# A graph network on one core: a GpSimd share of the one-hot rows, loads ahead of stores, and quarters of sums ahead of one-hot products

## The chip, the cores and the metric

The kernel runs on one core of a Trainium2 chip. The metric is the device time of one execution in microseconds, as the median of several runs. Times in a trace count from the start of the profiled span.

## What is computed

`x` holds 12,500 nodes of 64 numbers; `src` and `dst` hold 400,000 edges, sorted by `dst`. The reference, cut to what matters (the weights are 64 x 64, three layers):

```python
h = jnp.maximum(_layernorm(x, axis=-1), 0.0)
edge_index = jnp.stack([src, dst])          # row, col = src, dst
for l in range(3):
    mlp = lambda z: jnp.maximum(z @ W1[l] + b1[l], 0.0) @ W2[l] + b2[l]
    msgs = mlp(h[col])
    agg = segment_sum(msgs, row, num_segments=12500)
    h = mlp(h + agg)
return x + h @ Wf + bf
```

The message of a node depends on the node alone. So the sums over edges are a product of a matrix of counts (how many edges lead from one node to another) with the messages. The kernel builds that matrix once, two counts of four bits in a byte, stores it in DRAM, and multiplies it with the messages of each layer.

## The kernel before

**The build** is 49 steps (`BUILD`), j = 0 to 48, of four groups (`HG`), so 196 groups k = 4j + h. A step takes a window of 128 edges' keys per partition. For each group of 32 columns:

- VectorE, `make_hots(k)`: two comparisons (both through line 766): first the one-hot words of the columns (832 elements), then the one-hot rows, `hot_r` (128 elements for each of the 32 columns, 4096). From k = 32 on (`FEW_FROM`) ScalarE makes four of the 32 rows (`FEW`) and VectorE compares 28 (3584 elements). There are two slots (`SLOTS`), so that group k waits for TensorE's products of group k - 2.
- GpSimd, `weigh(k)` (line 643): multiplies the words with the edges' weights, as soon as the comparison of the words is done. After the third group of a step it issues an indirect DMA for a later window (line 628).
- TensorE, `multiply_group(k)` (line 1392): 32 one-hot products, in two halves of 16, each into two PSUM banks. It waits for `rows_made`, `few_made`, `hots_made`, and, by `batch_kept`, until the copies of group k - 1 are done.
- ScalarE, in this order for group k: at some k `keep_sums` (line 1208), at h = 0 `relate_rows`; then the distances of the next group's four rows (line 1183, four operations), the copy of the first half out of PSUM (line 1198), the next group's four rows (line 1189), the copy of the second half (line 1198), and `row_edges` (line 1201), which raises `batch_kept` by two. After groups 1 and 3 it copies the next step's keys (`keep_keys`).
- VectorE, `turn_counts(k)` (line 774), two groups later: transposes the copied counts into `ctile`, which has two slots; it waits until the store of group k - 2 has landed. SyncE then stores the group with four DMAs (line 467).

**The fused units.** From j = 8 on, each step also works on one unit of layer 0's sums, u = j - 8 (`unit_of`), 41 units in the build (`FUSED`) of 49 in all. A unit has two rounds of counts. SyncE loads each round (`load_round`, line 478), VectorE unpacks it in two halves (`unpack_low`, line 808, and `unpack_high`, line 813), and TensorE multiplies it in four quarters, `add_bank(u, h)` with h = 0 to 3 (line 1428, 28 matmuls each). Quarters 0 and 1 use the first round, 2 and 3 the second. From u = 7 on, quarter 0 is preceded by `add_kept` (line 1419, 8 matmuls), which puts the earlier sums back into PSUM. In each group TensorE's order is the one-hot products, then the group's quarter; at h = 1 `turn_keys` (lines 1364 and 1366) stands between them. Until k = 56 VectorE also makes parts of the messages (`lower_parts`, line 854).

**SyncE's queue** in step j: the stores of groups 4j - 2 and 4j - 1, the load of the next unit's first round, the store of group 4j, the load of its second round, the store of group 4j + 1. A load at the start of every seventh unit waits until all stores that it reads have landed.

**After the build** VectorE turns the last two groups and unpacks the rest of layer 0 (`unpack_tail`, lines 872 and 873), and the products of layer 0's last units, of layer 1 and of layer 2 follow. TensorE's `add_kept` for unit 41 is the first of these.

All engines are ordered by semaphores and by the order in which their instructions are issued.

Of the kernel before, what the change touches and what calls it, by code (L numbers as in the profile page):

```python
# [13 lines left out]
P = 128  # L14
# [14 lines left out]
HI = 32  # L29
# [39 lines left out]
FEW_FROM = 32  # L69
PITCH = 512 // 8  # L70
# [3 lines left out]
PSLOTS = 2  # L74
LAG = 2
# [43 lines left out]
def gnn_kernel(nc, x, src, dst, W1, b1, W2, b2, Wf, bf, out):  # L119
    ctx = ExitStack()  # L120
    with ctx:
# [52 lines left out]
        few_now = sb("few_now", [P, HG, FEW], F32)  # L174
# [57 lines left out]
        ctile, build_end = view(at, [2, HBYTES], U8)  # L232
        ring0, at = view(build_end, [RING0, CK * SBH], U8)
        spread, at = view(at, [WIDE, 2, CK * SBH], U8)
        win, at = view(at, [WR, 2 * WIN], I32)
# [25 lines left out]
        def kept_sums(st, b):  # L261
# [32 lines left out]
            "norm_made", "rows_relative", "keys_turned", "keys_kept", "cols_made", "rows_made", "few_far_found", "few_made", "hots_made",  # L294
            "batch_multiplied", "batch_kept", "counts_turned",
                        "counts_stored_0", "counts_stored_1",
# [15 lines left out]
        counts_stored = [s["counts_stored_0"], s["counts_stored_1"]]  # L312
# [106 lines left out]
        def _(sp):  # L419
# [41 lines left out]
            def store_counts(k):  # L461
                sp.wait_ge(s["counts_turned"], k + 1)
                j, h = k // HG, k % HG
                for d in range(2):
                    for r in range(HROWS):
                        q = (d * HROWS + r) * HI
                        sp.dma_start(counts_dram[j * 2 + d, h * HW:(h + 1) * HW, r * HBYTES:(r + 1) * HBYTES],  # L467
                                     ctile[q:q + HI, h % 2, :]).then_inc(counts_stored[h % 2], 16)

            def load_round(n):  # L470

                u, c = n // ROUND, n % ROUND
                if c == 0 and u % SB == 0:
                    for half in counts_stored:
                        sp.wait_ge(half, 64 * 2 * KG * (u // SB + 1))
# [6 lines left out]
            for j in range(BUILD):  # L482
                u = unit_of(j + 1)
                if j in (3, 6):
                    store_h0(j // 6)
                if j:
                    store_counts(j * HG - 2)
                    store_counts(j * HG - 1)
                if u >= 0:
                    load_round(ROUND * u)  # L490
                store_counts(j * HG)
                if u >= 0:
# [98 lines left out]
        def _(pool):  # L591
# [87 lines left out]
        def _(dve):  # L679
# [89 lines left out]
            def turn_counts(k):  # L769

                dve.wait_ge(s["batch_kept"], 2 * k + 2)
                if k >= 2:
                    dve.wait_ge(counts_stored[k % 2], 64 * (k // 2))
                v.transpose(ctile[:, k % 2, :].bitcast(I32), stage[:, k % 2, :].bitcast(I32)).then_inc(s["counts_turned"], 1)  # L774

            def make_hots(k):
# [8 lines left out]
                few = FEW if k >= FEW_FROM else 0  # L785
# [77 lines left out]
            def unpack_tail(n):  # L863
# [234 lines left out]
        def _(act):  # L1098
# [51 lines left out]
            def keep_keys(t, u):  # L1150
                if t:
                    act.wait_ge(s["rows_made"], (t - 1) * HG + 2 * u + 2)
                    act.wait_ge(s["hots_made"], (t - 1) * HG + 2 * u + 2)
                act.wait_ge(s["keys_turned"], t + 1)
# [3 lines left out]
                    "p (h c) -> p h c", h=2)[:, :, 0:FEW], ACT.Copy, scale=-1.0)  # L1158
# [17 lines left out]
            def find_few_distances(k):  # L1176
# [5 lines left out]
                for c in range(FEW):  # L1182
                    last = a.activation(few_far[:, c, :], row_iota[:], ACT.Abs, bias=few_now[:, k % HG, c:c + 1])  # L1183
                last.then_inc(s["few_far_found"], 1)

            def make_few_rows(k):

                act.wait_ge(s["few_far_found"], k - FEW_FROM + 1)
                a.activation(hot_r[:, k % SLOTS, 0:FEW, :], few_far[:], ACT.Relu, scale=-RK_UNIT, bias=1.0).then_inc(  # L1189
# [150 lines left out]
        def _(pe):  # L1340
# [133 lines left out]
            for k in range(BUILD * HG):  # L1474
# [21 lines left out]
                if unit_of(j) >= 0:  # L1496
# [159 lines left out]
```

## Time and profile before

| | us |
|---|---|
| median of 3 runs | 2127.72 (2125.79 to 2129.39) |
| the profiled execution | 2123.59 |
| its span | 2121.9 |
| TensorE busy with matmuls | 1957.8 (92%) |
| VectorE | 1403.5 (66%) |
| ScalarE | 869.8 (41%) |
| GpSimd | 551.1 (26%) |

The shares are means over stages that differ. The build with its fused units ends near 912 us; up to there VectorE, ScalarE and, from about 190 us on, TensorE all have work in every step. Behind it nearly all is TensorE. The time of an operation in a row can overlap that of the next on the same engine by some 0.1 us, so that the distance between two starts says better what one costs.

### The profile page before, as it was taken

The page shows a single profiled execution, that of the slowest core. Times are in us where ns is not written, and L with a number is a line of the kernel's source. Part 1 is how long each engine was busy: PE and PEld are TensorE (multiplying, and loading weights), DVE is VectorE, ACT ScalarE, POOL GpSimd, SP SyncE. Part 2 cuts the span into 40 slices and gives each one's busy share as a digit, 9 for nine tenths or more (in the row PEclk, how much of TensorE's full clock was granted, in tenths as well). Part 3 has the DMA queues.
Part 4 walks back from the last instruction along what each step waited for, and adds up shares of the span by engine and source line. Part 5 has one row for each costly group of instructions (what it writes and reads, how often), then busy time and mean ns, then how long its engine had stood idle before and what let it go on. Part 6 is the DMA issues. An engine that isn't in the chain of part 4 may idle for free.

```text
span 2121.9 us, 57789 instructions
## 1 busy us (share of the span) xinstructions
PE 1957.8 (92%) x24911; PEld 1194.8 (56%) x24911; DVE 1403.5 (66%) x1613; ACT 869.8 (41%) x2278; POOL 551.1 (26%) x270
## 2 busy tenths in 40 slices
PE   4656889999999999989999999999999999999998
PEld 3544555555555555555555555555555555555554
DVE  8999999999999999945543343343365433434333
ACT  5986999999989999922200000000010000000000
POOL 2666656666666665500000000000000000000000
PEclk9796999999999999999999999999999999999999
DMA  7356666667666666662544553543544555555452
GB/s 206 92 142 181 184 176 196 197 201 201 196 192 193 198 193 188 190 202 78 161 145 123 168 153 109 182 144 117 170 151 132 168 169 163 161 153 169 140 168 73
DMA packets 332933, 346.21 MB, mean 163 GB/s; under 512 B 21562, under 2 KB 303992, under 8 KB 332184
## 3 DMA queue, kind: packets, MB, share of 16 engines
q1 hardware_dynamic: 327516, 335.59, 54.1%
q0 software_dynamic: 2352, 6.43, 1.2%
q8 instruction: 198, 3.24, 0.7%
q10 hardware_dynamic: 2816, 0.53, 0.2%
q14 instruction: 51, 0.42, 0.1%
HBM read 252.58 MB, written 89.89 MB: 161 GB/s over the span
## 4 chain that ended last, share of the span: by engine, by line
PE 61%; DVE 20%; DMA 7%; issue 5%; ACT 3%; POOL 2%; SPq 2%; DVEq 0%; POOLq 0%; ACTq 0%
PE ps L1428 57%; DVE arena L766 10%; DMA arena<-counts_dram 6%; DVE arena L774 4%; POOL arena L643 2%; SPq L467 2%; DVE arena L808 2%; PE ps L1392 1%; DVE arena L813 1%; PE ps L1540 1%; PE ps L1512 1%; DMA counts_dram<-arena 1%; ACT arena L1198 1%; DVE arena L743 1%; ACT few_far L1183 1%
## 5 line engine op out<-in xcount | busy, mean ns | idle before, releaser
L1428 PE MATMUL ps<-arena,parts 128*64 128x448 fp8e4 x16464 | 1610.9, 354 | 3.8 <-DVE arena L901 1.9
L1428 PEld LDWEIGHTS ps<-arena,parts 128*64 128x64 f16 x16464 | 916.6, 110 | 655.7 <-issue 55.4
L888 DVE TENSOR_SCALAR arena<-arena 128x3136 uint16<-128x3136 uint16 x196 | 191.3, 976 | 574.7 <-PE ps L1428 574.7
L643 POOL TENSOR_TENSOR arena<-arena,weight_now 128x416 int32<-128x416 int32 x196 | 480.3, 2451 | 314.3 <-DVE arena L766 313.6
L1291 ACT ACTIVATE arena<-arena 128x448 f32<-128x448 f32 x42 | 23.9, 577 | 975.0 <-DVE arena L915 975.0
L766 DVE TENSOR_TENSOR arena<-row_iota,key_now 128x3584 f16<-128x3584 f16 (+1 forms) x196 | 403.6, 2059 | 0.0
L1198 ACT ACTIVATE arena<-ps 128x800 uint16<-128x800 f32 x392 | 342.7, 886 | 56.2 <-PE ps L1392 55.2
L1392 PE MATMUL ps<-arena 128*128 128x53 fp8e4 x6272 | 205.7, 190 | 104.9 <-POOL arena L643 88.9
L1392 PEld LDWEIGHTS ps<-arena 128*128 128x128 f16 x6272 | 187.7, 98 | 177.8 <-issue 93.2
L1183 ACT ACTIVATE few_far<-row_iota,few_now 128x128 f16<-128x128 f16 x656 | 214.1, 431 | 0.0
L774 DVE STREAM_TRANSPOSE arena<-arena 128x800 int32<-128x800 int32 x196 | 196.6, 1003 | 5.5 <-DMA counts_dram<-arena 5.5
L889 DVE TENSOR_SCALAR arena<-arena 128x3136 uint16<-128x3136 uint16 x196 | 190.0, 970 | 0.0
L634 POOL PARTITION_ALL_REDUCE scal<-scal x2 | 2.0, 1014 | 633.9 <-DVE scal L833 633.9
L656 POOL PARTITION_ALL_REDUCE good<-good x1 | 0.4, 409 | 557.4 <-DVE good L1041 557.4
L766 DVE TENSOR_TENSOR arena<-word_iota,key_now 128x832 uint16<-128x832 f16 x196 | 113.7, 580 | 0.0
L1189 ACT ACTIVATE arena<-few_far 128x512 f16<-128x512 f16 x164 | 103.6, 632 | 0.0
L808 DVE TENSOR_SCALAR arena<-arena 128x3136 uint16<-128x3136 uint16 x82 | 78.4, 956 | 18.2 <-DMA arena<-counts_dram 16.1
L813 DVE TENSOR_SCALAR arena<-arena 128x3136 uint16<-128x3136 uint16 x82 | 76.5, 933 | 0.0
L1242 ACT ACTIVATE parts<-msg,scal 128x448 f16<-128x448 f32 x42 | 26.2, 677 | 98.8 <-DVE msg L926 55.6
L628 POOL DMA_INDIRECT arena<-edges_dram,start_i x49 | 63.2, 1289 | 8.1 <-issue 6.3
L1208 ACT ACTIVATE msg<-ps 128x448 f32<-128x448 f32 x70 | 39.8, 569 | 27.6 <-PE ps L1428 27.6
L904 DVE TENSOR_SCALAR arena<-ps,scal 128x448 f32<-128x448 f32 x28 | 19.1, 684 | 42.7 <-PE ps L1428 42.6
(145 smaller groups left out, 841.7 us busy)
## 6 DMA issues: line engine op xcount, KB each, us to landing
arena<-counts_dram SPq DMA_DIRECT2D x294, 784.0 KB, 4.7
counts_dram<-arena SPq DMA_DIRECT2D x784, 100.0 KB, 2.3
h_dram<-parts SPq DMA_DIRECT2D x2, 1536.0 KB, 7.3
edges_dram<-arena SPq DMA_DIRECT2D x2, 1400.0 KB
arena<-in_x_dram SPq DMA_DIRECT2D x14, 192.0 KB
out_dram<-arena SPq DMA_DIRECT2D x14, 192.0 KB
arena<-in_dst_dram SPq DMA_DIRECT2D x1, 1400.0 KB
arena<-in_src_dram SPq DMA_DIRECT2D x1, 1400.0 KB
```

The costliest lines, as they stand in the source:

```text
L643: nc.gpsimd.tensor_tensor(pairs, pairs, weight_now[:, h * HW:(h + 1) * HW].unsqueeze(2).to_broadcast([P, HW, WORDS // 2]), ALU.mult).then_ ...
L766: return v.tensor_tensor(out, numbers.rearrange("p (m two) -> p m two", two=2).unsqueeze(1).to_broadcast(shape), key.unsqueeze(2).to_broad ...
L774: v.transpose(ctile[:, k % 2, :].bitcast(I32), stage[:, k % 2, :].bitcast(I32)).then_inc(s["counts_turned"], 1)
L808: v.tensor_scalar(spread[:, n % WIDE, 0, :].bitcast(U16), ring0[:, n % RING0, :].bitcast(U16), 0x0F0F, None, ALU.bitwise_and)
L813: v.tensor_scalar(spread[:, n % WIDE, 1, :].bitcast(U16), ring0[:, n % RING0, :].bitcast(U16), 4, 0x0F0F, ALU.logical_shift_right, ALU.bit ...
L888: v.tensor_scalar(spread[:, c % WIDE, 0, :].bitcast(U16), packed, 0x0F0F, None, ALU.bitwise_and)
L889: v.tensor_scalar(spread[:, c % WIDE, 1, :].bitcast(U16), packed, 4, 0x0F0F, ALU.logical_shift_right, ALU.bitwise_and).then_inc(s["counts_ ...
L1183: last = a.activation(few_far[:, c, :], row_iota[:], ACT.Abs, bias=few_now[:, k % HG, c:c + 1])
L1189: a.activation(hot_r[:, k % SLOTS, 0:FEW, :], few_far[:], ACT.Relu, scale=-RK_UNIT, bias=1.0).then_inc(s["few_made"], 1)
L1198: a.activation(to, product(q)[:, :, 0:2 * LP].rearrange("p c (m two) -> p c m two", two=2), ACT.Copy, scale=1.0 / WEIGHT_UNIT)
L1392: last = t.matmul(product(q)[:, c, 0:COLS], hot_r[:, slot, w, :], hot_c8[:, slot, w, 0:COLS], start=True, stop=True)
L1428: last = t.matmul(ps[half(c), b, 0:NB], parts[:, tile, half(part)], spread[:, wide, c ^ exchange, at:at + NB].bitcast(F8), start=start and ...
```

## The change

- `BY_POOL = 1`: GpSimd makes one of the 32 one-hot rows of every group, by a new `match_row(k)`, one `tensor_scalar` of 128 elements. It is issued behind `weigh(k - 1)` and ahead of the gather. VectorE compares 31 columns, and 27 from k = 32 on; ScalarE's four move up by one, and `few_now` holds five numbers per group.
- `TURNED = 3`: `ctile` has three slots, so `turn_counts(k)` waits for the store of group k - 3.
- SyncE: except at units that open a row of seven, both rounds of the next unit are loaded ahead of the stores of groups 4j - 2 and 4j - 1.
- TensorE: at h = 1, 2 and 3 the quarter of sums stands ahead of the group's one-hot products. At h = 0 it stays behind them.
- Behind the build, one unpacking stands ahead of the last `turn_counts`, and it waits for `chunks_multiplied` where it waited for `sums_done`.
- The windows of keys (`win`) move to the end of the arena.

```diff
+BY_POOL = 1
+TURNED = 3
-        few_now = sb("few_now", [P, HG, FEW], F32)
+        few_now = sb("few_now", [P, HG, BY_POOL + FEW], F32)
-        ctile, build_end = view(at, [2, HBYTES], U8)
+        ctile, build_end = view(at, [TURNED, HBYTES], U8)
...
                 u = unit_of(j + 1)
+                opens = u >= 0 and u % SB == 0
+                if u >= 0 and not opens:
+                    load_round(ROUND * u)
+                    load_round(ROUND * u + 1)
                 if j:
                     store_counts(j * HG - 2)
                     store_counts(j * HG - 1)
-                if u >= 0:
+                if opens:
                     load_round(ROUND * u)
                 store_counts(j * HG)
-                if u >= 0:
+                if opens:
                     load_round(ROUND * u + 1)
                 store_counts(j * HG + 1)
...
+            def match_row(k):
+
+                pool.wait_ge(s["keys_kept"], k // 2 + 1)
+                if k >= SLOTS:
+                    pool.wait_ge(s["batch_multiplied"], 2 * (k - SLOTS) + 2)
+                nc.gpsimd.tensor_scalar(hot_r[:, k % SLOTS, 0, :], row_iota[:], few_now[:, k % HG, 0:1], 0.0, ALU.add,
+                                        ALU.is_equal).then_inc(s["pool_rows_made"], 1)
+
+            match_row(0)
             for k in range(BUILD * HG):
                 weigh(k)
+                if k + 1 < BUILD * HG:
+                    match_row(k + 1)
...
-                if k >= 2:
-                    dve.wait_ge(counts_stored[k % 2], 64 * (k // 2))
-                v.transpose(ctile[:, k % 2, :].bitcast(I32), stage[:, k % 2, :].bitcast(I32)).then_inc(s["counts_turned"], 1)
+                if k >= TURNED:
+                    dve.wait_ge(counts_stored[k % TURNED], 64 * (k // TURNED))
+                v.transpose(ctile[:, k % TURNED, :].bitcast(I32), stage[:, k % 2, :].bitcast(I32)).then_inc(s["counts_turned"], 1)
...
-                few = FEW if k >= FEW_FROM else 0
+                few = BY_POOL + (FEW if k >= FEW_FROM else 0)
...
                 if c == 0 and u > FUSED:
                     dve.wait_ge(s["counts_used"], u - FUSED)
+                elif c == 0:
+                    dve.wait_ge(s["chunks_multiplied"], u)
                 else:
                     dve.wait_ge(s["sums_done"], SBB * u)
...
-            for k in range(BUILD * HG - LAG, BUILD * HG):
-                turn_counts(k)
+            turn_counts(BUILD * HG - 2)
             unpack_tail(ROUND * FUSED)
+            turn_counts(BUILD * HG - 1)
             unpack_tail(ROUND * FUSED + 1)
...
+                    act.wait_ge(s["pool_rows_made"], (t - 1) * HG + 2 * u + 2)
...
+                pe.wait_ge(s["pool_rows_made"], k + 1)
                 pe.wait_ge(s["hots_made"], k + 1)
...
+                if unit_of(j) >= 0 and h:
+                    add_bank(unit_of(j), h)
                 multiply_group(k)
...
-                if unit_of(j) >= 0:
+                if unit_of(j) >= 0 and not h:
                     add_bank(unit_of(j), h)
```

## Rows read from the trace of the kernel before

**Rows 1.** Windows: us, then busy time of each engine, clock, DMA share, GB/s.

```profile
core 0: us, PE busy (x) PEld busy (x) DVE busy (x) ACT busy (x) POOL busy (x), PEclk, DMA share, GB/s
250.00:350.00 100.00, 88.51 (x1356) 55.22 (x1354) 98.32 (x96) 90.32 (x238) 62.65 (x29) 0.97 0.64 185
1000.00:1500.00 500.00, 498.06 (x5544) 291.24 (x5544) 215.29 (x269) 34.83 (x62) 1.68 (x1) 1.00 0.49 146
```

**Rows 2.** Timeline of PE, G0 of four steps: start, duration, idle before and releaser.

```profile
191.06 1.60 PE L1392 MATMUL ps<-arena 128*128 128x53 fp8e4 x32 [2.91 <-POOL arena L643]
...
321.63 0.99 PE L1392 MATMUL ps<-arena 128*128 128x53 fp8e4 x32 [0.60 <-POOL arena L643]
...
878.41 0.99 PE L1392 MATMUL ps<-arena 128*128 128x53 fp8e4 x32 [0.38 <-ACT row_edges L1201]
...
895.28 0.89 PE L1392 MATMUL ps<-arena 128*128 128x53 fp8e4 x28 [0.39 <-ACT row_edges L1201]
```

**Rows 3.** Waits from 250 to 860 us: who for whom, us in total, times, longest.

```profile
PE ps L1392 <- POOL arena L643: 39.3, 69, 2.7
...
DVE arena L808 <- DMA arena<-counts_dram: 15.7, 21, 2.1
...
PE ps L1392 <- ACT row_edges L1201: 9.4, 29, 1.1
```

**Rows 4.** Timeline of PE, one step and the start of the next.

```profile
601.88 0.99 PE L1392 MATMUL ps<-arena 128*128 128x53 fp8e4 x32 [0.28 <-ACT row_edges L1201]
602.80 0.98 PE L1419 MATMUL ps<-msg,ident 64*64 64x448 f32 x8
603.72 2.84 PE L1428 MATMUL ps<-arena,parts 128*64 128x448 fp8e4 x28
606.64 0.99 PE L1392 MATMUL ps<-arena 128*128 128x53 fp8e4 x32
...
607.73 2.84 PE L1428 MATMUL ps<-arena,parts 128*64 128x448 fp8e4 x28
610.50 1.01 PE L1392 MATMUL ps<-arena 128*128 128x53 fp8e4 x32
...
614.21 1.01 PE L1392 MATMUL ps<-arena 128*128 128x53 fp8e4 x32
...
618.27 0.99 PE L1392 MATMUL ps<-arena 128*128 128x53 fp8e4 x32 [0.29 <-ACT row_edges L1201]
```

**Rows 5.** Timeline of PE and of ACT, G2 of step 48 and its first copy.

```profile
904.32 0.99 PE L1392 MATMUL ps<-arena 128*128 128x53 fp8e4 x32 [0.48 <-POOL arena L643]
...
904.99 0.88 ACT L1198 ACTIVATE arena<-ps 128x800 uint16<-128x800 f32 x1 [0.87 <-PE ps L1392]
```

**Rows 6.** Timeline of ACT, from `keep_sums` to `row_edges` of one group.

```profile
614.32 0.54 ACT L1208 ACTIVATE msg<-ps 128x448 f32<-128x448 f32 x1 [0.86 <-PE ps L1428]
614.76 1.27 ACT L1183 ACTIVATE few_far<-row_iota,few_now 128x128 f16<-128x128 f16 x4
615.93 0.85 ACT L1198 ACTIVATE arena<-ps 128x800 uint16<-128x800 f32 x1
...
617.94 0.19 ACT L1201 ACTIVATE row_edges<-ps 128x32 f16<-128x32 f32 x1
```

**Rows 7.** Timeline of DVE, row comparisons of both forms.

```profile
183.41 2.28 DVE L766 TENSOR_TENSOR arena<-row_iota,key_now 128x4096 f16<-128x4096 f16 x1
...
188.03 2.02 DVE L766 TENSOR_TENSOR arena<-row_iota,key_now 128x3584 f16<-128x3584 f16 x1
```

**Rows 8.** Timeline of POOL: scaling of `row_iota`, and one `weigh` behind a gather.

```profile
15.28 0.75 POOL L612 TENSOR_SCALAR row_iota<-row_iota 128x128 f16<-128x128 f16 x1
...
611.59 1.84 POOL L643 TENSOR_TENSOR arena<-arena,weight_now 128x416 int32<-128x416 int32 x1
```

**Rows 9.** Timeline of DVE, the row comparison beside that `weigh`.

```profile
610.66 2.01 DVE L766 TENSOR_TENSOR arena<-row_iota,key_now 128x3584 f16<-128x3584 f16 x1
```

**Rows 10.** Timeline of DVE and of PE, the end of the build.

```profile
914.08 1.01 DVE L774 STREAM_TRANSPOSE arena<-arena 128x800 int32<-128x800 int32 x1 [4.00 <-DMA counts_dram<-arena]
...
916.94 1.75 PE L1419 MATMUL ps<-msg,ident 64*64 64x448 f32 x8 [5.15 <-DVE arena L873]
```

More of the change, by code:

```diff
@@ L231, in gnn_kernel @@
         stage, at = view(at, [2, HBYTES // 2], U16)
-        ctile, build_end = view(at, [2, HBYTES], U8)
+        ctile, build_end = view(at, [TURNED, HBYTES], U8)
         ring0, at = view(build_end, [RING0, CK * SBH], U8)
         spread, at = view(at, [WIDE, 2, CK * SBH], U8)
-        win, at = view(at, [WR, 2 * WIN], I32)
+        win, at = view(ARENA - WR * 2 * WIN * 4, [WR, 2 * WIN], I32)
         assert at <= ARENA
@@ L293, in gnn_kernel @@
             "vector_chain", "variance_made", "root_made", "h0_made", "h0_stored", "h0_turned", "h0_kept",
-            "norm_made", "rows_relative", "keys_turned", "keys_kept", "cols_made", "rows_made", "few_far_found", "few_made", "hots_made",
+            "norm_made", "rows_relative", "keys_turned", "keys_kept", "cols_made", "rows_made", "few_far_found", "few_made", "pool_rows_made", "hots_made",
             "batch_multiplied", "batch_kept", "counts_turned",
-                        "counts_stored_0", "counts_stored_1",
+                        "counts_stored_0", "counts_stored_1", "counts_stored_2",
             "hidden0_done", "hidden0_kept", "message0_done", "message_kept",
@@ L311, in gnn_kernel @@
         counts_loaded = [sem(f"counts_loaded_{r}") for r in range(RING)]
-        counts_stored = [s["counts_stored_0"], s["counts_stored_1"]]
+        counts_stored = [s["counts_stored_0"], s["counts_stored_1"], s["counts_stored_2"]]
         chain = [0]
@@ L467, in store_counts @@
                         sp.dma_start(counts_dram[j * 2 + d, h * HW:(h + 1) * HW, r * HBYTES:(r + 1) * HBYTES],
-                                     ctile[q:q + HI, h % 2, :]).then_inc(counts_stored[h % 2], 16)
+                                     ctile[q:q + HI, k % TURNED, :]).then_inc(counts_stored[k % TURNED], 16)
             def load_round(n):
@@ L473, in load_round @@
                 if c == 0 and u % SB == 0:
-                    for half in counts_stored:
-                        sp.wait_ge(half, 64 * 2 * KG * (u // SB + 1))
+                    groups = HG * KG * (u // SB + 1)
+                    for slot in range(TURNED):
+                        sp.wait_ge(counts_stored[slot], 64 * len(range(slot, groups, TURNED)))
                 if n >= RING0:
@@ L1157, in keep_keys @@
                 a.activation(few_now[:, 2 * u:2 * u + 2, :], key_bank[:, 0, u * P // 2:(u + 1) * P // 2].rearrange(
-                    "p (h c) -> p h c", h=2)[:, :, 0:FEW], ACT.Copy, scale=-1.0)
+                    "p (h c) -> p h c", h=2)[:, :, 0:BY_POOL + FEW], ACT.Copy, scale=-1.0)
                 a.copy(weight_now[:, u * P // 2:(u + 1) * P // 2], key_bank[:, 2, u * P // 2:(u + 1) * P // 2]).then_inc(
@@ L1182, in find_few_distances @@
                 for c in range(FEW):
-                    last = a.activation(few_far[:, c, :], row_iota[:], ACT.Abs, bias=few_now[:, k % HG, c:c + 1])
+                    last = a.activation(few_far[:, c, :], row_iota[:], ACT.Abs, bias=few_now[:, k % HG, BY_POOL + c:BY_POOL + c + 1])
                 last.then_inc(s["few_far_found"], 1)
@@ L1188, in make_few_rows @@
                 act.wait_ge(s["few_far_found"], k - FEW_FROM + 1)
-                a.activation(hot_r[:, k % SLOTS, 0:FEW, :], few_far[:], ACT.Relu, scale=-RK_UNIT, bias=1.0).then_inc(
+                a.activation(hot_r[:, k % SLOTS, BY_POOL:BY_POOL + FEW, :], few_far[:], ACT.Relu, scale=-RK_UNIT, bias=1.0).then_inc(
                     s["few_made"], 1)
```

## The prediction

> **What bounds the kernel now.** The windows come first [rows 1]. From 1000 us on TensorE is busy 498.06 of 500 us and GpSimd 1.68: that half has no one-hot work, and no edit reaches it. In the build three engines are nearly full at once: of 100 us VectorE works 98.32, ScalarE 90.32, TensorE 88.51. A small shift can change which of them sets the pace, so the stage has to be read step by step.
>
> Call the four one-hot products of a step G0 to G3 (32 matmuls each) and the four quarters of sums B0 to B3 (28 each). The starts of G0 in four steps are anchors [rows 2]: G0 of the first fused step (k = 32) at 191.06, of the first step with `add_kept` (k = 60) at 321.63, of k = 188 at 878.41 and of k = 192 at 895.28. The first stretch is 7 steps in 130.57 us, 18.65 each; the second 33 steps in 573.65 us, 17.38 each. An undisturbed step takes 895.28 - 878.41 = 16.87. The 0.51 above that in the mean is stalls: in the table of waits of the build, VectorE sat 15.7 us for loads of counts (21 times), TensorE 39.3 us for GpSimd and 9.4 us for ScalarE's copies [rows 3]. The pace of 16.87 is VectorE's.
>
> One whole step of TensorE follows in order of time [rows 4]. G0 to `add_kept` 602.80 - 601.88 = 0.92; `add_kept` 603.72 - 602.80 = 0.92; B1 610.50 - 607.73 = 2.77, and the other quarters the same when nothing is waited for; G1 with `turn_keys` 607.73 - 606.64 = 1.09; G2 with B2 614.21 - 610.50 = 3.71, so G2 alone 0.94, and G3 too. TensorE's own work in a step is 0.92 + 0.92 + 4 x 2.77 + 1.09 + 0.94 + 0.94 = 15.89 us. Against 16.87 it has 1 us to spare.
>
> **The part that decides: the order on TensorE.** Before: G0 B0 G1 B1 G2 B2 G3 B3, then the next G0. After: G0 B0 B1 G1 B2 G2 B3 G3, then the next G0. No matmul is added. But now G3 and the next step's G0 stand side by side, with no quarter between. G(k+1) may not begin until ScalarE has copied G(k) out of PSUM: `multiply_group` waits for `batch_kept`, which line 1201 raises after both halves. Before, a quarter of 2.77 us lay over every such copy; now three of four are covered, G0's by two quarters, and G3's by none.
>
> The length of the uncovered copy: where ScalarE stood idle, it began the first copy 904.99 - 904.32 = 0.67 us after its group began [rows 5]. From the start of the first copy, over the 4-row activation, the second copy and `row_edges`, to the start of the next G was 618.27 - 615.93 = 2.34 us [rows 4, 6]. So at least 3.01 us from G3's start to the next G0's. Is ScalarE free in time? Count from G2's start in the new order: its copies are done at 0.67 + 2.34 - 0.14 = 2.87 (the last 0.14 being the way from the end of `row_edges`, 618.13, to the matmul). Then `keep_sums` takes 614.76 - 614.32 = 0.44 and the four distances 615.93 - 614.76 = 1.17 [rows 6], so the first copy of G3 can begin at 4.48. G3 starts at 0.94 + 2.77 = 3.71, and 3.71 + 0.67 = 4.38 is sooner: ScalarE is 0.10 late. From G3 to the next G0 it is 3.11 us, of which G3 fills 0.94.
>
> New step of TensorE: 15.89 - 0.94 + 3.11 = **18.06 us**, and nothing can make it shorter while the copies take this long. The hole is 2.17 us. It has no cover. Over 33 steps: 33 x 18.06 - 573.65 = **+22.3 us**.
>
> Does another engine need still more? VectorE's pace becomes 16.60 (below). In the new order G1 starts 0.92 + 0.92 + 5.54 = 7.38 after G0, some 3 us later than now, and `make_hots` of group 3 waits for it (two slots). That gives VectorE a start at about 8.45; by its own work it then reaches the next G0's one-hots ready 0.8 after 15.1, before 18.06. The quarters need the counts unpacked about 17 us after G0 and use them at 19.9. So VectorE idles about 1.2 us per step, and the engine that becomes late next is TensorE with ScalarE in turn.
>
> **The 32nd of the rows.** VectorE compares 27 (early 31) columns for 28 (32). The form of 4096 elements takes 2.28 us and that of 3584 2.02 [rows 7]: 0.26 for four columns, 0.065 for one. Per step 0.26, hence 16.87 - 0.26 = 16.60. In the 33 steps this is hidden under the hole and worth nothing. In the 32 groups in front of the fused steps, where VectorE is the bound, 32 x 0.065 = 2.1 us.
>
> GpSimd gets one operation of 128 f16 elements per group. The nearest row is its scaling of `row_iota`, same shape: 0.75 us [rows 8]. It runs behind `weigh(k)` and ahead of the gather and `weigh(k+1)`. `weigh` ran 1.84 us from 611.59, ending 0.76 after the comparison of VectorE that began at 610.66 (2.01 us long), so GpSimd's product finishes only after VectorE's row comparison, however early it begins [rows 8, 9]. A start 0.1 to 0.7 later costs little, and group 1 to 3 now have 3 to 4 us of room in TensorE's order. What the trace does not show is whether the added operation holds VectorE up. Nothing to 0.75 us per group; I take a small loss, since during `weigh` and the gather VectorE's operations keep their length: the prologue as a whole gives -1 (from -2.1 to +22, the latter a rival below). The two waits added, ScalarE's in `keep_keys` and TensorE's in `multiply_group`, are for an event that comes before `hots_made` of the same group and block nothing more. `few_now` grows from 8 to 10 elements: nothing.
>
> **Loads in front of stores, three slots.** A load of counts is issued about half a step earlier, behind stores that are already out; the eight to twelve DMAs of `store_counts` that it passes are held back by one or two loads, which the third slot pays for. It can remove the 15.7 us of VectorE's waits for loads [rows 3]. In the 33 steps it is, again, worth nothing, since VectorE has slack there: that gain is already lost in 18.06 against 17.38. In the 7 early steps (`lower_parts` runs on VectorE until k = 56, and `add_kept` doesn't exist yet) TensorE needs 18.06 - 0.92 = 17.14, and VectorE stays the bound at 18 or a little less: 18.65 - 18.1 = 0.5 per step, less for the steps with the weights' products: **-2.5** (from 0 to -7).
>
> **The seam.** After the last group VectorE waited 4.00 us for a store before its last transpose (914.08), and TensorE 5.15 us (`add_kept` at 916.94) for the unpacking behind it [rows 10]. With a third slot and the unpacking in front of the last transpose this goes. From G0 (895.28) to 916.94 it was 21.66. New: 0.92 + 0.92 + 5.54 + 0.83 + 2.77 + 0.94 + 2.77 = 14.7 to G3, then its copies without the few rows (2.36), `keep_sums` 0.58 and 0.15: 17.8. What is late next is the load of unit 42, which needs all stores and may cost 1. The seam gives **-4** (from -1.5 to -6.6).
>
> **Sum.** +22.3 - 1 - 2.5 - 4 = +14.8 us. The profiled execution of before took 2123.6 us (span 2121.9), 4.1 under the median of the runs, 2127.7. 2123.6 + 14.8 = 2138.4; against the median **2142.5**.
>
> **The rivals.** *A, VectorE's pace after all (faster).* If the hole did not open, because G3's copies were covered by something, each step would go at 16.60: 33 x 16.60 - 573.65 = -25.9, with the rest -33: 2094. For it: TensorE lost only about 0.3 us per step to ScalarE, and 39.3 us to GpSimd, which quarters ahead of the products do cover. Against it: those 0.3 us remained behind a full quarter of 2.77 [rows 4]. It decides if G3 to G0 takes under about 2.5 us (a step of 17.5). Chance 0.12.
>
> *B, no difference.* The hole opens, 0.15 shorter (+17), and the rest comes out at its best ends: -2.1, -7, -6.6: +1, 2129. It needs three bounds at once: 0.08.
>
> *C, GpSimd's comparison holds VectorE.* If each cost VectorE the 0.75 us of its row [rows 8], its step would be 16.60 + 4 x 0.75 = 19.6, over TensorE's 18.06: 33 x 19.6 - 573.65 = +73, prologue 32 x 0.685 = +22, early steps 7 x (18.1 + 3.0 - 18.65) = +17, seam -4: 2236. It decides from 0.37 us per group. Against it: the comparison that ran beside `weigh` took 2.01 us, no longer than the one of the build's start (2.02) [rows 7, 9]. The Trainium skill (SBUF — State Buffer, section "SBUF: two separate sides") has this rule: the port pair that VectorE and GpSimd share is an exclusive lock, whoever starts first has it for its whole instruction. By that rule a comparison on GpSimd that begins just before VectorE's next one blocks it; the tail of 0.76 us of `weigh` fits the rule seen from the other side, GpSimd being the one shut out. Chance 0.06.
>
> The forecast has 0.74. Its own range: in the window of 250 to 350 us, with TensorE busy 88.51%, the granted clock was 0.97 [rows 1]; a busy share of 15.89 / 18.06 = 88% could see the same, 3% of 15.89 us in 33 steps = +16: 2158. Downwards it ends where B begins, 2128. That range, with B, holds 8 in 10; A and C lie outside. Within 0.2% (4.3 us, about what a measurement of this kernel can tell from no change) 0.08, faster 0.12, slower 0.74 + 0.06 = 0.80.
>
> **What would show it.** In the changed kernel's timeline of TensorE: one G per step with about 2.1 us idle ahead of it, released by `row_edges` of ScalarE, and the waits for that line up from 9.4 to 75 or 90 us, those for GpSimd nearly gone; G0 to G0 even at 18.06; VectorE's busy share down from 98% to about 92%, idle behind TensorE's G1; its waits for loads nearly gone; the end from 1000 us on unchanged. It would be wrong if the next G0 starts less than 3 us behind G3, if its wait is named for GpSimd or VectorE, or if VectorE's operations grow longer beside GpSimd's comparison.

## The result and the profile after

| | before | after |
|---|---|---|
| median of runs | 2128.19 us (4 runs) | 2192.32 us (4 runs, 2188.19 to 2200.55) |
| ratio | 1 | 1.0308, 95% interval 1.0274 to 1.0341 |
| profiled execution | 2123.59 us | 2194.78 us |
| its span | 2121.9 us | 2192.9 us |

The change makes the kernel 64 us slower. The sign and one of the mechanisms were forecast, but less than a quarter of the size: 2142.5 was predicted and the range ended at 2158.

One step of TensorE in the changed kernel, in order of time, as [rows 4] for before (line 1414 is now the one-hot products, 1441 `add_kept`, 1450 the quarters, 1222 `row_edges`):

```profile
642.91 1.20 PE L1414 MATMUL ps<-arena 128*128 128x53 fp8e4 x32 [2.32 <-ACT row_edges L1222]
644.04 1.77 PE L1441 MATMUL ps<-msg,ident 64*64 64x448 f32 x8
645.75 6.04 PE L1450 MATMUL ps<-arena,parts 128*64 128x448 fp8e4 x56
651.72 1.01 PE L1414 MATMUL ps<-arena 128*128 128x53 fp8e4 x32
...
655.60 1.01 PE L1414 MATMUL ps<-arena 128*128 128x53 fp8e4 x32
...
659.31 1.01 PE L1414 MATMUL ps<-arena 128*128 128x53 fp8e4 x32
662.60 0.99 PE L1414 MATMUL ps<-arena 128*128 128x53 fp8e4 x32 [2.29 <-ACT row_edges L1222]
```

The reader should see two things. Between G3 (659.31) and the next G0 (662.60) lies the forecast hole, 2.29 us, released by `row_edges`. And behind the hole the same matmuls take longer: `add_kept` 1.71 us from start to start where [rows 4] has 0.92, and the two quarters 5.97 where twice 2.77 are 5.54. The windows of the same kernel say why (us, busy time of each engine, granted clock, DMA share, GB/s):

```profile
643.00:646.00 3.00, 3.00 (x42) 1.46 (x43) 3.00 (x4) 3.00 (x12) 1.53 (x2) 0.58 1.09 364
646.00:650.00 4.00, 4.00 (x40) 2.27 (x38) 4.00 (x5) 2.67 (x8) 3.49 (x3) 0.89 0.48 112
650.00:660.00 10.00, 10.00 (x170) 6.42 (x166) 8.44 (x8) 7.25 (x20) 8.38 (x5) 1.00 0.42 101
```

For the first 3 us behind the hole the granted clock is 0.58 of full speed, for the most part its lower level of 1.2 GHz; later it is 1.00, 2.4 GHz.

The table of waits from 250 to 900 us, as [rows 3], which end at 860 us: ScalarE's copies now hold TensorE for 76.2 us, GpSimd for 5.3 us, and loads hold VectorE for 1.6 us.

```profile
PE ps L1414 <- ACT row_edges L1222: 76.2, 34, 3.0
...
PE ps L1414 <- POOL arena L651: 5.3, 2, 3.0
...
DVE arena L827 <- DMA arena<-counts_dram: 1.6, 3, 0.6
```

The anchors, as [rows 2] and [rows 10], from the timeline of TensorE: G0 of k = 32, 60 and 192, and `add_kept` of unit 41.

```profile
192.95 1.24 PE L1414 MATMUL ps<-arena 128*128 128x53 fp8e4 x24 [2.47 <-POOL arena L651]
...
337.16 0.99 PE L1414 MATMUL ps<-arena 128*128 128x53 fp8e4 x32 [2.13 <-ACT row_edges L1222]
...
969.31 0.99 PE L1414 MATMUL ps<-arena 128*128 128x53 fp8e4 x32 [2.12 <-ACT row_edges L1222]
...
987.10 0.98 PE L1441 MATMUL ps<-msg,ident 64*64 64x448 f32 x8 [2.04 <-ACT msg L1229]
```

Subtracted from each other and compared with before:

| stretch | before, us | after, us | difference | forecast |
|---|---|---|---|---|
| to G0 of k = 32 | 191.06 | 192.95 | +1.9 | -1 |
| k = 32 to 60, 7 steps | 130.57 | 144.21 | +13.6 | -2.5 |
| k = 60 to 192, 33 steps | 573.65 | 632.15 | +58.5 | +22.3 |
| the seam, to `add_kept` of unit 41 | 21.66 | 17.79 | -3.9 | -4 |
| the rest of the span | 1204.96 | 1205.8 | +0.8 | 0 |

The differences add up to the 71.0 us between the two profiled spans. The medians differ by 64, since the profiled execution before was 4.6 us under its median and the one after 2.5 us over. The +1.9 of the first stretch says nothing: in `order_only` below, which has the code of before up to k = 32, G0 of k = 32 starts at 192.27, and in other runs at 188.8 to 194.8.

### The profile page after: what moved, and what is told of

It reads as the page before. It is cut to its first block, busy times and chain, and to the rows that moved or that the text cites. A ratio compares the mean times of both kernels' runs of the same rounds, so it can differ in the third digit from the quotient of the medians.

```text
span 2192.9 us, 58312 instructions
## 1 busy us (share of the span) xinstructions
PE 1990.2 (91%) x24911; PEld 1210.9 (55%) x24911; DVE 1447.0 (66%) x1613; ACT 867.3 (40%) x2278; POOL 810.2 (37%) x466
## 4 chain that ended last, share of the span: by engine, by line
PE 72%; DVE 10%; ACT 8%; issue 5%; POOL 3%; DMA 1%; SPq 0%; ACTq 0%; DVEq 0%; POOLq 0%
PE ps L1450 62%; DVE arena L785 4%; PE ps L1414 4%; ACT arena L1219 3%; DVE arena L793 2%; PE ps L1441 2%; POOL arena L660 2%; ACT arena L1210 1%; ACT few_far L1204 1%; PE ps L1565 1%; DVE arena L832 1%; PE ps L1537 1%; ACT parts L1158 1%; POOL arena L636 1%; DMA arena<-in_src_dram 1%
## 5 line engine op out<-in xcount | busy, mean ns | idle before, releaser
L1450 PEld LDWEIGHTS ps<-arena,parts 128*64 128x64 f16 x16464 | 928.6, 111 | 685.2 <-issue 88.7
L909 DVE TENSOR_SCALAR arena<-arena 128x3136 uint16<-128x3136 uint16 x196 | 191.3, 976 | 574.6 <-PE ps L1450 574.6
L651 POOL TENSOR_TENSOR arena<-arena,weight_now 128x416 int32<-128x416 int32 x196 | 371.7, 1896 | 81.3 <-DVE arena L785 80.1
L785 DVE TENSOR_TENSOR arena<-row_iota,key_now 128x3456 f16<-128x3456 f16 (+1 forms) x196 | 393.6, 2008 | 0.0
L660 POOL TENSOR_SCALAR arena<-row_iota,few_now 128x128 f16<-128x128 f16 x196 | 347.3, 1772 | 47.9 <-PE ps L1414 41.5
L910 DVE TENSOR_SCALAR arena<-arena 128x3136 uint16<-128x3136 uint16 x196 | 190.1, 970 | 0.0
L785 DVE TENSOR_TENSOR arena<-word_iota,key_now 128x832 uint16<-128x832 f16 x196 | 129.5, 661 | 37.2 <-PE ps L1414 37.2
L827 DVE TENSOR_SCALAR arena<-arena 128x3136 uint16<-128x3136 uint16 x82 | 93.4, 1138 | 8.4 <-PE ps L1450 6.7
L832 DVE TENSOR_SCALAR arena<-arena 128x3136 uint16<-128x3136 uint16 x82 | 95.6, 1166 | 0.0
L636 POOL DMA_INDIRECT arena<-edges_dram,start_i x49 | 88.0, 1796 | 8.4 <-issue 5.9
L1441 PE MATMUL ps<-msg,ident 64*64 64x448 f32 x280 | 47.0, 749 | 2.0 <-ACT msg L1229 2.0
```

The lines of the kernel that those rows point to most:

```text
L651: nc.gpsimd.tensor_tensor(pairs, pairs, weight_now[:, h * HW:(h + 1) * HW].unsqueeze(2).to_broadcast([P, HW, WORDS // 2]), ALU.mult).then_ ...
L660: nc.gpsimd.tensor_scalar(hot_r[:, k % SLOTS, 0, :], row_iota[:], few_now[:, k % HG, 0:1], 0.0, ALU.add, ALU.is_equal).then_inc(s["pool_ro ...
L785: return v.tensor_tensor(out, numbers.rearrange("p (m two) -> p m two", two=2).unsqueeze(1).to_broadcast(shape), key.unsqueeze(2).to_broad ...
L832: v.tensor_scalar(spread[:, n % WIDE, 1, :].bitcast(U16), ring0[:, n % RING0, :].bitcast(U16), 4, 0x0F0F, ALU.logical_shift_right, ALU.bit ...
L909: v.tensor_scalar(spread[:, c % WIDE, 0, :].bitcast(U16), packed, 0x0F0F, None, ALU.bitwise_and)
L910: v.tensor_scalar(spread[:, c % WIDE, 1, :].bitcast(U16), packed, 4, 0x0F0F, ALU.logical_shift_right, ALU.bitwise_and).then_inc(s["counts_ ...
```

## The experiments

All times are medians beside runs of the kernel before on the same chip. These had a median of 2125.2 beside order_only to no_pool_row, 2129.1 beside loads_only to hole_filled_no_pool_row and 2126.2 beside the last two, so across these sets the ratios compare better than the times. "Mean step" is that of the 33 steps from k = 60 to 192, each from G0 to G0, in the one profiled execution of each kernel.

| kernel | us | ratio to before, 95% interval | mean step | typical single steps |
|---|---|---|---|---|
| before | | 1 | 17.38 | 16.87, some up to 20.3 |
| after | 2192.3 | 1.0308 (1.0274 to 1.0341) | 19.16 | 18.2 and 19.8 |
| order_only | 2181.0 | 1.0246 (1.0224 to 1.0268) | 18.65 | 17.90 and 19.54 |
| old_order | 2141.2 | 1.0072 (1.0055 to 1.0089) | 18.02 | 18.15 |
| hole_filled | 2157.1 | 1.0146 (1.0129 to 1.0163) | 18.17 | 18.16 |
| no_pool_row | 2172.5 | 1.0220 (1.0203 to 1.0237) | 18.65 | 17.90 and 19.53 |
| loads_only | 2106.9 | 0.9900 (0.9874 to 0.9927) | 16.97 | 16.86 |
| pool_row_only | 2149.2 | 1.0097 (1.0069 to 1.0125) | 18.03 | 18.15 |
| all_quarters_first | 2243.1 | 1.0540 (1.0512 to 1.0569) | 20.51 | 20.5 |
| hole_filled_no_pool_row | 2148.9 | 1.0094 (1.0065 to 1.0122) | 17.95 | 17.93 |
| all_first_sums_kept | 2109.0 | 0.9914 (0.9882 to 0.9946) | 16.97 | 16.86 |
| gather_at_h0 | 2121.3 | 0.9974 (0.9961 to 0.9987) | 17.33 | 17.30 |

**order_only: TensorE's order alone.** The kernel before, with

```diff
+                if unit_of(j) >= 0 and h:
+                    add_bank(unit_of(j), h)
                 multiply_group(k)
...
-                if unit_of(j) >= 0:
+                if unit_of(j) >= 0 and not h:
                     add_bank(unit_of(j), h)
```

> The kernel before with TensorE's new order alone (quarters 1 to 3 of a unit ahead of the group's one-hot products). Theory H (the uncovered copy of G3 leaves TensorE idle 2.3 us in every step, and the granted clock falls after many of these holes): almost the whole loss is here, 2185 to 2200 us, steps alternating near 18.2 and 19.8. Rival P (GpSimd's row comparison and VectorE take the port from each other and this is what lengthens the steps): 2145 to 2160, the hole's +22 us alone. VectorE's operations as short as before in either case.

Measured 2181.0, just under theory H's band and far over rival P's. The order alone costs 2.5%. Its steps come in two lengths, 18 of 17.7 to 18.0 (mean 17.89) and 15 of 19.5 to 19.7 (mean 19.57). TensorE's timeline has one of each kind of hole:

```profile
649.44 1.01 PE L1392 MATMUL ps<-arena 128*128 128x53 fp8e4 x32
652.49 0.99 PE L1392 MATMUL ps<-arena 128*128 128x53 fp8e4 x32 [2.04 <-ACT row_edges L1201]
653.42 1.45 PE L1419 MATMUL ps<-msg,ident 64*64 64x448 f32 x8
654.80 6.66 PE L1428 MATMUL ps<-arena,parts 128*64 128x448 fp8e4 x56
...
672.03 0.99 PE L1392 MATMUL ps<-arena 128*128 128x53 fp8e4 x32 [2.05 <-ACT row_edges L1201]
672.96 0.98 PE L1419 MATMUL ps<-msg,ident 64*64 64x448 f32 x8
673.87 5.49 PE L1428 MATMUL ps<-arena,parts 128*64 128x448 fp8e4 x56
```

and its windows the clock behind each:

```profile
653.00:656.00 3.00, 3.00 (x35) 1.21 (x33) 3.00 (x3) 3.00 (x9) 2.50 (x1) 0.63 0.16 40
...
672.00:675.00 3.00, 2.97 (x52) 1.83 (x54) 3.00 (x3) 3.00 (x11) 2.43 (x1) 1.00 0.31 72
```

G3 to the next G0 is 652.49 - 649.44 = 3.05 us, 3.11 in the prediction. Both holes are the same length, 2.04 and 2.05. Behind the first the granted clock was 0.63 for 3 us, and `add_kept` and the two quarters took (661.39 - 653.42) 7.97 us; behind the second it was 1.00, and they took (679.29 - 672.96) 6.33. The 1.64 us between them is the whole difference between 19.54 and 17.90.

**old_order: everything but TensorE's order.** The changed kernel with that diff undone.

> The changed kernel with TensorE's order as before; GpSimd's row, loads first, the third slot and the new end of the build stay. Theory H: VectorE's pace; its operations are longer beside GpSimd (some 0.6 us per step net), the stalls for loads are gone (-17) and the end of the build gives up to -4: 2095 to 2130. Rival P: 2160 or more, since what slows is still there.

Measured 2141.2, in neither band. The order is worth 51 of the 64 us, but what stays is slower than before too. The first 28 of the 33 steps took 18.1 to 18.2 us (but for one of 18.88 and the next of 17.42), with VectorE busy 398.15 of 400 us and the clock at 1.00:

```profile
400.00:800.00 400.00, 355.09 (x5530) 219.26 (x5529) 398.15 (x354) 350.56 (x927) 352.06 (x200) 1.00 0.65 188
```

So VectorE's pace is no longer 16.87 or 16.60, and the clock has nothing to do with it. One step's VectorE and GpSimd beside each other (line 785 are the comparisons, 793 the transpose, 827 and 832 the unpacking; on GpSimd 651 is `weigh`, 660 the new row, 636 the gather):

```profile
643.15 1.00 DVE L793 STREAM_TRANSPOSE arena<-arena 128x800 int32<-128x800 int32 x1
644.08 1.85 DVE L827 TENSOR_SCALAR arena<-arena 128x3136 uint16<-128x3136 uint16 x1
...
649.25 1.08 DVE L832 TENSOR_SCALAR arena<-arena 128x3136 uint16<-128x3136 uint16 x1
...
640.55 0.72 POOL L660 TENSOR_SCALAR arena<-row_iota,few_now 128x128 f16<-128x128 f16 x1
641.42 2.73 POOL L636 DMA_INDIRECT arena<-edges_dram,start_i  x1 [0.15 <-DVE arena L785]
644.18 0.91 POOL L651 TENSOR_TENSOR arena<-arena,weight_now 128x416 int32<-128x416 int32 x1
...
649.14 1.33 POOL L660 TENSOR_SCALAR arena<-row_iota,few_now 128x128 f16<-128x128 f16 x1
```

The unpacking beside the product of 0.91 us takes 1.85 us, 0.92 more than the 0.93 of an undisturbed one (a row of loads_only has 0.92, one of pool_memset 0.94). The one beside the row takes 1.08, 0.15 more. The row and the gather have pushed one of the step's four `weigh` out from beside VectorE's row comparison, where it waited and cost nothing, to a place where it holds VectorE.

The same run has the test of this in it. The gather runs six windows ahead of 49 (`k // HG + WR < WT`), so from step 43 on there is none. The last five steps took 17.2 to 17.4, and none of their unpackings took over 1.1 us; two starts of G0 from there:

```profile
900.15 1.00 PE L1414 MATMUL ps<-arena 128*128 128x53 fp8e4 x32 [0.38 <-ACT row_edges L1222]
...
917.40 1.00 PE L1414 MATMUL ps<-arena 128*128 128x53 fp8e4 x32 [0.39 <-ACT row_edges L1222]
```

**hole_filled: work in the hole.**

```diff
                     add_bank(unit_of(j), h)
+                if k >= 48 and h == 0:
+                    for _ in range(30):
+                        t.matmul(ps[:, 2, 0:P], ident16[:], ident16[:], start=True, stop=True)
                 multiply_group(k)
```

> The changed kernel; ahead of each G0 from k = 48 on, TensorE makes 30 extra products of the identity with itself into an unused PSUM bank (some 1.8 us of work where it idled; the result is not used). Theory H, its part on the clock: no step near 19.8 is left, all near 18.2, the granted clock 1.00, 25 to 35 us less than the changed kernel: 2157 to 2167. Rival (the long steps come from VectorE, ScalarE or GpSimd): no gain, 2190 to 2210.

Measured 2157.1, at the lower end of theory H's band: 35 us less for 30 useless matmuls per step. One step near 19.8 is left of 20, where G0 waited 1.78 us for GpSimd and the next step was 17.54, and the granted clock over 400 to 800 us is 1.00, from 0.95. More work on TensorE made the kernel faster, so the clock's fall is a cost of the idle time and not of something that happens to lie beside it. The steps stay at 18.16, which old_order shows to be VectorE's pace.

**no_pool_row: the changed kernel without GpSimd's row.** `BY_POOL = 0`, no `match_row`, no wait for it.

> The changed kernel without GpSimd's row: VectorE compares 32 and 28 columns again. Theory H: TensorE with ScalarE stays the bound, VectorE's extra 0.27 us per step is hidden: 2185 to 2195. Rival P: the long steps go, 2145 to 2165.

Measured 2172.5, in neither band: 20 us less than the changed kernel, so the row is not hidden under the hole as theory H had it; and only a third of the loss, so rival P is no account of the whole either. The steps are those of order_only, 17.90 and 19.53. The row adds 0.51 to the mean step, in two ways. It lifts the short steps from 17.90 to VectorE's 18.15 and the long ones from 19.57 (order_only) to 19.81, which is half of it. The other half is that more steps are long: 20 of 33 in the changed kernel, 15 in order_only. The hole grows with it: in most steps it is 2.27 to 2.35 us with the row, 2.02 to 2.08 without. In the last five steps, which have no gather, the steps of the changed kernel are those of order_only, 18.02 and 19.66 against 18.03 and 19.65: there the row costs nothing.

**loads_only: loads first, three slots, the new end of the build.** The changed kernel without GpSimd's row and with TensorE's order as before.

> The kernel before with loads first, three slots and the new end of the build; no GpSimd row, TensorE's order as before. Theory H: VectorE's pace of 16.87 us with the stalls for loads gone (33 x 0.51 = 17 us), the end of the build 4 us shorter, early steps up to 4 shorter: 2100 to 2108. Rival D (the loads, issued in front, hold the stores back, and the waits move from loads to stores): 2118 to 2130.

Measured 2106.9, 1.0% faster than before, inside theory H's band. The steps are 16.86 with few exceptions, a mean of 16.97. By the trace 13.6 us are gained in the 33 steps (560.02 for 573.65) and 4.4 at the seam (17.30 for 21.66). Which of the three edits earns what in the steps was not told apart. This part of the change is good; in the whole change it is covered by the rest. It has the lowest time of the study, with all_first_sums_kept 2 us behind, a difference inside the intervals.

**pool_row_only: GpSimd's row alone**, in the kernel before.

> The kernel before with GpSimd's row alone. In the changed kernel with the old order every step took 18.15 us with VectorE busy all the time, against 16.87 without stalls before. If GpSimd's row is the cause, this kernel has steps of 18.15 too: 33 x (18.15 - 17.38) = +25, less what of the stalls for loads hides behind it, and +2 to +6 ahead: 2150 to 2160. If loads first or the third slot was the cause (stores and loads colliding), it is 2120 to 2130.

Measured 2149.2, 1 us under the band of the row as the cause and far over the other; steps of 18.15 as in old_order. The row alone makes VectorE's pace 18.15, with stores and loads in their old order too. It costs 20 us here, and 34 to 37 where VectorE has no other stalls (old_order less loads_only: 2141.2 - 2106.9, or 1.72% by the ratios).

**all_quarters_first: the first quarter in front as well.** In loads_only:

```diff
+                if unit_of(j) >= 0:
+                    add_bank(unit_of(j), h)
+                if k == FUSE_AT + 1:
+                    multiply_weights()
                 multiply_group(k)
...
-                if unit_of(j) >= 0:
-                    add_bank(unit_of(j), h)
```

> As loads_only, but all four quarters of a unit stand ahead of the group's one-hot products, the first too, so that a quarter lies between every two groups; the weights' products stand behind the quarter. Theory H: no copy is uncovered, no hole, clock 1.00, VectorE's pace: 2098 to 2108. Rival E (to have a quarter ahead of products is bad in itself, since the slots come free later and VectorE waits for TensorE): over 2120.

Measured 2243.1, a plain miss. A quarter stands between all groups, and still there is a hole, now ahead of `add_kept` (line 1436 in this kernel):

```profile
620.73 1.01 PE L1409 MATMUL ps<-arena 128*128 128x53 fp8e4 x32
624.68 1.77 PE L1436 MATMUL ps<-msg,ident 64*64 64x448 f32 x8 [2.94 <-ACT msg L1225]
626.38 3.60 PE L1445 MATMUL ps<-arena,parts 128*64 128x448 fp8e4 x28
```

`add_kept` waits for `keep_sums` (line 1225), and in ScalarE's order `keep_sums` of the second bank stands behind the copies of G3 and the keys. TensorE waits for the same copies by another semaphore, 2.94 us and not 2.05, and the clock falls behind this hole in nearly every step: 1.70 us for `add_kept` here where 0.92 is usual.

**all_first_sums_kept.** The same, with ScalarE's order changed so that those sums are kept ahead of the copies of G3. The lines that kept them later are taken out:

```diff
-                if k and unit_of((k - 1) // HG) >= 0 and b >= 0:
+                if k and unit_of((k - 1) // HG) >= 0 and b == 0:
...
+                if h == HG - 1 and unit_of(j) >= 0:
+                    keep_sums(unit_of(j), SBB - 1)
                 keep_batch(2 * k)
...
-            keep_sums(FUSED - 1, SBB - 1)
```

> As all_quarters_first (2243), but ScalarE keeps the second sums of a unit (keep_sums for b = 1) ahead of the copies of G3 and no longer behind them, so that add_kept doesn't wait for these copies. Theory H (an uncovered copy of ScalarE is the cause there too, by way of sums_kept): the wait of 2.95 us ahead of add_kept goes, VectorE sets the pace again: 2100 to 2115. Rival E (quarters ahead of products cost by themselves, through the slots): still over 2150.

Measured 2109.0, in theory H's band: 134 us less by the place of one ScalarE operation per step. Steps of 16.86 again, VectorE busy 396.33 of 400 us. So a quarter ahead of the products is no harm in itself; what harms is a copy that nothing covers. It is no faster than loads_only, since VectorE sets the pace in both.

**hole_filled_no_pool_row: the two together.** The changed kernel without GpSimd's row and with the 30 matmuls in the hole.

> The changed kernel without GpSimd's row, and with the 30 extra products in the hole. Theory H: only the hole itself is left, every step at 17.90 and none near 19.5: 33 x (18.65 - 17.90) = 25 us and some us ahead less than without GpSimd's row and unfilled (2172.5): 2140 to 2148. If the extra products don't help here, 2165 or more.

Measured 2148.9, 1 us over the band; all steps 17.7 to 18.1, most of them 17.93. This is the pure price of the uncovered copy, 17.93 against the 16.86 of loads_only, with the clock kept up and GpSimd out of the way.

**gather_at_h0: GpSimd's gather two groups earlier**, in old_order: `if k % HG == 0` for `if k % HG == 2`.

> As old_order, but GpSimd issues the gather behind its first product of a step and not behind the third. In old_order one unpacking per step took 1.85 us and not 0.93, beside a product of GpSimd that the row and the gather had pushed behind VectorE's row comparison. Theory P (a late product of GpSimd holds VectorE): that 0.9 us goes and the pace is 17.2 to 17.4, 2141 - 33 x 0.85 = 2110 to 2118. If the displaced product isn't the cause: 18.1 and 2138 to 2145 as before.

Measured 2121.3, 20 us less than old_order; the total is 3 us over the band, the step of 17.30 is inside it. The unpacking of 1.85 us is gone (1.08 in its place). All four `weigh` of a step lie beside row comparisons again. The remaining 17.30 - 16.60 is the row itself: the four unpackings of a step are 0.09 to 0.15 us longer from start to start than in pool_memset below, and one comparison of the words 0.12.

**pool_memset: zeros for the row.** In old_order GpSimd fills its row with zeros and the comparison is left out.

> As old_order (2141, steps of 18.15), but GpSimd only fills its row with zeros and reads nothing; the comparison is left out. Lock by reading and writing alike: VectorE's unpacking is still held up by each of them, steps above 17.6. Lock only while GpSimd reads, or merely its length: the fill takes 0.2 us or less, ends inside VectorE's transpose, GpSimd is on time for the next product again: steps of 16.6 to 16.9, 2098 to 2112.

With one row of each group empty the kernel's own count of the edges comes out short and it goes through its general path as well, 104385 us in all; only the build, ahead of that, can be read. There the single steps are 16.60 us, inside the second band and the pace that the prediction worked out for VectorE. The fill takes 0.20 us and ends inside the transpose, and the next product is on time:

```profile
640.58 1.01 DVE L792 STREAM_TRANSPOSE arena<-arena 128x800 int32<-128x800 int32 x1
641.51 0.94 DVE L831 TENSOR_SCALAR arena<-arena 128x3136 uint16<-128x3136 uint16 x1
...
641.37 0.20 POOL L660 MEMSET arena<- 128x128 f16 x1
643.09 2.49 POOL L651 TENSOR_TENSOR arena<-arena,weight_now 128x416 int32<-128x416 int32 x1 [1.52 <-DVE arena L784]
```

Whether it is harmless because it reads nothing or because it is short was not told apart.

## Why the prediction was right and wrong

Two terms of the sum failed in the 33 steps: the clock, which was put at nothing there, and the hold of GpSimd on VectorE, which was said to be hidden. And a wait early in the build was not in the sum at all. The uncovered copy, the main mechanism of the forecast, is there as worked out.

**The hole was right.** G3 and the next G0 stand side by side with ScalarE's copies uncovered in each step, and all but one of the 33 holes are released by `row_edges` as forecast. 3.11 us was worked out from G3 to G0; 3.05 was measured in order_only and 3.29 in the changed kernel (662.60 - 659.31). 18.06 was worked out for the step, and 17.90 measured where nothing else disturbs it. Over 33 steps the hole alone is 33 x (17.90 - 17.38) = 17 us, 22.3 in the sum. That the short steps of the changed kernel (18.15) are so near 18.06 is luck: their length is VectorE's, not the hole's.

**The clock was mis-sized.** The prediction left it out of the sum and put +16 into the range, by taking the mean clock of 0.97 of a 100 us window [rows 1]. What happens is no mean: behind about every second hole of 2.05 us the clock stands near 0.6 for 3 us, and the step is 1.64 longer. In order_only that is 33 x (18.65 - 17.90) = 25 us, as much as the hole and more; in the changed kernel it is 33 us (632.15 for the 33 steps, 599.45 in hole_filled). A row of before hinted at it, behind a longer idle time: `add_kept` takes 1.75 us behind 5.15 us [rows 10], at a granted clock of 0.53 from 916.9 to 918.7, and 0.98 without an idle time [rows 4].

**GpSimd's row was put on the wrong side.** Rival C, with a chance of 0.06, had the right pair of engines and part of the mechanism. It was said to decide from 0.37 us per group, and the row costs (18.15 - 16.60) / 4 = 0.39; but most of this comes by the `weigh` that the row and the gather displace (0.92 of 1.55 us per step), which rival C did not have. One sign of being wrong that the prediction named, VectorE's operations growing longer, came true. What failed is the evidence against the rival. The row comparison of VectorE that ran beside `weigh` was no longer than others [rows 7, 9], which is true, and it stays 1.95 us after the change: there VectorE was first, and GpSimd waited. The price lies where GpSimd is first, and before the change its product ended inside the transpose, so that no row of before shows it. That GpSimd ended 0.76 us after VectorE's comparison is in [rows 8, 9]; the row and the gather had to go behind that, where the unpacking follows the transpose, and this was not laid side by side. The Trainium skill's rule (SBUF — State Buffer, section "SBUF: two separate sides"), by which the first of the two holds the shared ports for its whole instruction, was quoted and given too little weight. For the product the trace agrees with it in size: 0.91 us of GpSimd, 0.92 us more of VectorE. The changed kernel has cases in which the product started sooner:

```profile
619.57 1.15 DVE L785 TENSOR_TENSOR arena<-word_iota,key_now 128x832 uint16<-128x832 f16 x1 [0.41 <-PE ps L1414]
...
623.43 1.43 DVE L832 TENSOR_SCALAR arena<-arena 128x3136 uint16<-128x3136 uint16 x1
...
619.31 0.91 POOL L651 TENSOR_TENSOR arena<-arena,weight_now 128x416 int32<-128x416 int32 x1
...
623.08 0.89 POOL L651 TENSOR_TENSOR arena<-arena,weight_now 128x416 int32<-128x416 int32 x1
```

What was left of the product at VectorE's start is 0.65 and 0.54 us, and VectorE's two operations are 0.57 and 0.50 longer than 0.58 and 0.93. Beside the row the trace does not agree: in old_order the row started at 649.14 and took 1.33, the unpacking started at 649.25, and it lost 0.15 and not the row's length. Whether the row holds the ports for a part of its time only, or its record is longer than its work, was not found out.

**The sum of the 33 steps.** Taken in one order, the hole gives 17, the clock 25 and the row 33 x (19.16 - 18.65) = 17 us, together about the 58.5 of the table. But half of the row's 17 comes as more steps at the lower clock. With the clock kept up the times of the 33 steps are 573.65 before, 592.36 with the hole (hole_filled_no_pool_row) and 599.45 with the row too (hole_filled), and 632.15 is the changed kernel: 18.7 for the hole, 7.1 for the row, 32.7 for the clock.

**A step was missing.** Early on the prediction gave -2.5 and it was +13.6. The weights' products at k = 39 wait for a ScalarE copy made after group 38. Before, the quarter of group 38 lay between; now it stands ahead, and TensorE waits 3.82 us, 0.48 before, and then works at the lower clock (the quarter behind takes 5.38 us where 2.84 is usual). The first line is of the kernel before:

```profile
225.00 0.49 PE L1468 MATMUL ps<-W1b,uS 128*128 128x128 f32 x2 [0.48 <-ACT uS L1214]
...
232.49 0.80 PE L1490 MATMUL ps<-W1b,uS 128*128 128x128 f32 x2 [3.82 <-ACT uS L1235]
...
235.54 5.38 PE L1450 MATMUL ps<-arena,parts 128*64 128x448 fp8e4 x28
```

From k = 32 to 40, in which this lies beside two holes, order_only lost (240.68 - 192.27) - (230.38 - 191.06) = 9 us, and the changed kernel (243.87 - 192.95) - 39.32 = 11.6 of its 13.6. The prediction had VectorE as the bound in these steps, with TensorE at 17.14; the lower clock was left out here too. Whoever moves a block past a wait must look at every wait that it had covered, the single ones too.

**The seam was right:** 17.8 us worked out, 17.79 measured; what came last was `keep_sums` (987.10, released by line 1229), as in the sum. The exact hit has some luck in it: the clock stayed up behind that hole, and in no_pool_row, with the same end of the build, it did not and the seam took 19.28. **Loads first was right:** the 15.7 us of VectorE's waits for loads were said to go, and to be worth nothing as long as TensorE is late; loads_only gains 13.6 us in the 33 steps, and in the changed kernel VectorE waited 1.6 us for loads and gained nothing by it. **The room of VectorE was half right:** it did idle behind TensorE, 30.4 us from 250 to 900 us, but in the short steps GpSimd's hold took all of it.

**Rival A** did not come about: nothing covers G3's copies. Neither did rival B, by which all would have cancelled out.

What stays open: why the clock falls behind only about every second of holes of equal length. The rows of order_only hold a hint: in its long steps from 504 to 728 us `add_kept` takes 1.77, 1.73, 1.64, 1.57, 1.45, 1.35 and 1.24 us one after the other, behind equal holes and in steps of nearly equal length; then come two short steps, and it is 1.77 again. So the lower clock sets in a little later each time, and the hole alone does not fix the moment. The counts of long steps come from one execution each, and the four runs of the changed kernel differ by 12 us with mean clocks of 0.953 to 0.961. Why the long steps of the changed kernel are 19.8 and not 19.57 was not followed further than to GpSimd's row.

## What to carry to other kernels

When two blocks of work change places on an engine, write down for each wait which block covered it before and which does after; the one pair that ends side by side sets the loss, and semaphores that come by another way (here `keep_sums`) can open the same hole again. An idle time of 2 us on TensorE cost its length and, behind about every second one, 1.64 us more at the lower clock, so a pace worked out from full-speed rows is a lower bound. Work moved from VectorE to GpSimd has to be placed against VectorE's instructions one by one: here a product beside a comparison that was first was free, and one in front of an unpacking cost VectorE the product's full length. It can also push the work behind it, which was free before, to such a place.

## What the runs showed of the hardware

- In order_only, behind an idle time of 2.04 us on TensorE the granted clock was 0.63 over 3 us, behind one of 2.05 us in the next step 1.00. Thirty small matmuls in the hole (hole_filled) kept it at 1.00 and took 35 us off the kernel.
- GpSimd's `tensor_scalar` of 128 f16 elements took 0.71 to 2.91 us, by what VectorE did beside it; a fill of the same size (pool_memset) 0.20 us.
- VectorE's unpacking of 3136 elements took 0.93 us alone, 1.08 beside GpSimd's row, 1.85 beside its product of 0.91 us (old_order).
